# A two-layer gated cross-attention model on one core: heads in pairs, one clip for two heads, float32 weighing in the first layer

## The reference, cut to what matters

```
x = x + tanh(g_xattn[0]) * L0_xattn(layernorm(x), ctx)     # 16 heads of 16
x = x + tanh(g_ffn[0])   * L0_ffn(layernorm(x))            # 8 experts, 3 rotations expm(gens), gate
x = x + tanh(g_xattn[1]) * L1_xattn(layernorm(x), ctx)     # 16 heads of 64
x = x + tanh(g_ffn[1])   * L1_ffn(layernorm(x))            # shared expert + 8 experts

L0_xattn: q, k, v = x@Wq+bq, c@Wk+bk, c@Wv+bv;  attn = softmax(clip(q@k.T/4, -10000, 10000))
          out = (attn @ v) @ Wo + bo
L1_xattn: q, k, v with low-rank additions, from context rows 0..370;  out = softmax(q@k.T/8) @ v
          out += softmax(q@ki.T/8) @ vi    # rows 371..374 with weights Wk_ipa, Wv_ipa
          out = out @ Wo + bo + low-rank part
```

## Time and profile before

| | |
|---|---|
| median of 3 runs (range) | 1279.41 us (1277.0 to 1284.21) |
| profiled execution: span from first to last instruction | 1277.4 us |
| PE (TensorE) busy, matmul | 1066.5 us, 83% |
| PEld (weight loads) busy | 746.0 us, 58% |
| DVE (VectorE) busy | 948.8 us, 74% |
| ACT (ScalarE) busy | 567.6 us, 44% |
| POOL (GpSimd) busy | 268.6 us, 21% |

### The profile page before, as it was taken

The page is one execution under the profiler, slowest core; times in us unless marked ns, Lnnn a source line. Parts: engine busy times, 40 slices in busy tenths (PEclk is TensorE's granted clock), DMA queues, the critical chain, the costliest instruction groups (busy, mean ns, idle before and its releaser), DMA issues.

```text
span 1277.4 us, 23029 instructions
## 1 busy us (share of the span) xinstructions
PE 1066.5 (83%) x7860; PEld 746.0 (58%) x7860; DVE 948.8 (74%) x2024; ACT 567.6 (44%) x1276; POOL 268.6 (21%) x303
## 2 busy tenths in 40 slices
PE   0688888882979999854688988998897699999997
PEld 0577777771634555643367877777776455455553
DVE  5588888897398888697567777777776667776775
ACT  3366666672433343441455556555555233222220
POOL 1422222202245563001000000000000013433331
PEclk9899999995699999896799999999998699999999
DMA  5000000001112122320000000000000231112100
GB/s 190 1 2 2 1 0 0 0 1 66 64 48 84 58 96 67 110 71 28 6 1 2 2 2 1 1 0 1 1 1 1 100 129 64 64 64 72 70 1 29
DMA packets 9935, 47.82 MB, mean 37 GB/s; under 512 B 1513, under 2 KB 3313, under 8 KB 6930
## 3 DMA queue, kind: packets, MB, share of 16 engines
q1 hardware_dynamic: 9874, 47.03, 10.7%
HBM read 45.92 MB, written 1.11 MB: 37 GB/s over the span
## 4 chain that ended last, share of the span: by engine, by line
PE 33%; DVE 30%; issue 20%; ACT 9%; POOL 5%; DMA 2%; DVEq 1%; ACTq 0%; POOLq 0%
PE pb L1119 8%; PE pb L1134 7%; POOL qz L1227 5%; DVE ST L844 4%; DVE ST L855 3%; DVE nm L850 3%; PE pb L640 2%; PE pb L613 2%; PE pb L597 2%; DVE ST L847 2%; ACT ST L728 2%; PE pb L1424 2%; PE pb L576 1%; ACT V L711 1%; PE pb L570 1%
## 5 line engine op out<-in xcount | busy, mean ns | idle before, releaser
L1119 PE MATMUL pb<-xT,KT 128*128 128x448 f16 x1248 | 244.2, 354 | 2.7 <-DVE qz L1197 2.7
L1227 POOL TENSOR_TENSOR qz<-qz,Z 128x448 f32<-128x448 f32 x128 | 169.1, 1331 | 286.8 <-ACT qz L1166 197.5
L1119 PEld LDWEIGHTS pb<-xT,KT 128*128 128x128 f16 x1248 | 121.6, 98 | 119.6 <-DVE qz L1197 5.8
L613 PE MATMUL pb<-KT,qz 128*112 128x375 f16 (+1 forms) x768 | 171.8, 334 | 3.2 <-POOL qz L921 2.1
L640 PE MATMUL pb<-V,ST 125*112 125x32 f16 (+1 forms) x1536 | 127.0, 214 | 53.2 <-DVE ST L855 52.9
L1134 PE MATMUL pb<-V,KT 128*128 128x448 f16 x816 | 162.6, 357 | 8.9 <-DVE V L1206 8.9
L640 PEld LDWEIGHTS pb<-V,ST 125*112 125x112 f16 x1536 | 109.9, 133 | 71.3 <-DVE ST L855 47.2
L736 ACT ACTIVATE ST<-pb 125x336 f16<-125x336 f32 x256 | 113.6, 444 | 45.1 <-PE pb L623 42.5
L855 DVE SCALAR_TENSOR_TENSOR ST<-pb,ST 125x336 f16<-125x336 f32 x256 | 127.7, 499 | 6.0 <-ACT ST L736 5.4
L1134 PEld LDWEIGHTS pb<-V,KT 128*128 128x128 f16 x816 | 80.3, 99 | 86.3 <-DVE V L1206 10.5
L623 PE MATMUL pb<-identf,ST 112*125 112x112 f32 x768 | 125.8, 273 | 1.6 <-ACT ST L728 1.6
(11 more groups left out here) (196 smaller groups left out, 1594.0 us busy)
## 6 DMA issues: line engine op xcount, KB each, us to landing
ST<-in_moe SPq DMA_DIRECT2D x9, 1536.0 KB, 7.8
ST<-in_moe SPq DMA_DIRECT2D x8, 1024.0 KB, 6.8
Z<-wd_scratch SPq DMA_DIRECT2D x16, 448.0 KB, 4.4
ST<-in_ctxT SPq DMA_DIRECT2D x4, 750.0 KB, 4.9
ST<-in_gens SPq DMA_DIRECT2D x2, 768.0 KB, 4.7
ST<-in_lora SPq DMA_DIRECT2D x2, 624.0 KB, 8.7
ST<-in_w1q SPq DMA_DIRECT2D x1, 1024.0 KB
ST<-in_w1k SPq DMA_DIRECT2D x1, 1024.0 KB
```

Source lines behind the costliest of these rows:

```text
L613: mm = pe.matmul(SB_[st % 2][0:S, 0:L.keys], qz[:, bs % 2, qa, h, :], kT[bs % 2][qb][:, h // L.per_tile, 0:L.keys], start=(n == 0), stop=( ...
L1119: mm = pe.matmul(banks[m % len(banks)][:, 0:HT], MW[:, es % 2, qa, c:c + 128], xT[:, qb, k, half * HT:(half + 1) * HT], start=(i == 0), st ...
L1227: pool.tensor_tensor(tile, tile, wdB[:, es % 2, half * HT:(half + 1) * HT], ALU.mult)\
```

## The change

- Heads go in pairs everywhere: both score banks belong to one pair (`SP2`), both transpose banks likewise (`TP2`). TensorE's order in a step is turn of pair p-1, units, weigh of pair p-2, units, scores of pair p+1.
- Layer 1's scores use 64 rows of the array: the two heads of a pair have different halves of the rows, and their matmuls alternate.
- Layer 0: the second clip takes both heads in one instruction; the transposed weights stay float32, written by one ScalarE instruction for both heads, and `lo` is gone there. V is float32 in `V0`, with a 17th column of ones for each head, so that the weighing itself gives the sums; the exponential has no sum. `weigh` is three float32 matmuls of 17 columns for a head, and `normalise` a reciprocal and a multiplication from PSUM. V's units are cut by VectorE alone.
- Layer 1: one maximum, one `hi` and one `lo` for both heads; `normalise` adds the halves in one reduction, and GpSimd divides (`divide`). The factor 16 (`OS`) moves to the `t` unit.
- `at` and `out_at` have new places, SBUF places shift.

```diff
-NORM_LAG = (3, 3)
+NORM_LAG = 2
@@ Layer
-            at = {0: 0, 1: 3, 2: 5, 3: 7, 4: 9, 5: 11}
-            out_at = {0: 5, 1: 8}
+            at = {0: 1, 1: 3, 2: 5, 3: 7, 4: 9, 5: 11}
+            out_at = {0: 5, 1: 13}
...
+            at = dict(enumerate((1, 1, 2, 3, 3, 4, 5, 6, 7, 7, 8, 12, 13, 13, 14, 15, 15)))
+            out_at = {0: 5, 1: 9, 2: 11}
+        order = [0, 4, 1, 5, 2, 6, 3, 7]
+        self.order = list(range(H)) if index else order + [8 + h for h in order]
+        self.pairs = [self.order[2 * p:2 * p + 2] for p in range(NP)]
@@ scores
-                if st >= 2:
-                    pe.wait_ge(s["mx_done0"] if l == 0 else s["exp_done1"], i - 1)
+                if st >= 1:
+                    pe.wait_ge(s["mx_done0"] if l == 0 else s["exp_done1"], 2 * i)
                 for n, (qa, qb) in enumerate(PARTS):
-                    mm = pe.matmul(SB_[st % 2][0:S, 0:L.keys], qz[:, bs % 2, qa, h, :],
-                                   kT[bs % 2][qb][:, h // L.per_tile, 0:L.keys], start=(n == 0), stop=(n == 2))
+                    for j, h in enumerate(L.pairs[p]):
+                        if l == 0:
+                            t, r = h // 8, slice(0, 128)
+                            q = qz[:, bs % 2, qa, h, :]
+                        else:
+                            t, r = h // 2, slice(64 * (h % 2), 64 * (h % 2) + 64)
+                            q = qz[r, bs % 2, qa, h, :]
+                        mm = pe.matmul(SB_[j][0:S, 0:L.keys], q, kT[bs % 2][qb][r, t, 0:L.keys],
+                                       start=(n == 0), stop=(n == 2))
@@ turn
+                if st >= 1:
+                    pe.wait_ge(s["lo_done1"] if l else s["hi_done0"], i)
@@ weigh, layer 0
+                            mm = pe.matmul(psum_out(L, gs, h), PT0[:, st % 2, j, c * S:(c + 1) * S],
+                                           V0[0:CHUNK, bs % 2, c, h, :], start=(c == 0), stop=(c == NCH - 1))
@@ batch of TensorE
-                for h in range(H):
-                    scores(bv, bs, h)
-                    if bs or h >= 2:
-                        turn(bv * H + h - 2, bs * H + h - 2)
...
+                for p in range(NP):
+                    if bs or p >= 1:
+                        turn(bv * NP + p - 1, bs * NP + p - 1)
...
+                    if p >= 2:
+                        weigh(bv, bs, p - 2)
...
+                    if p < NP - 1:
+                        scores(bv, bs, p + 1)
@@ exps, hi
+                    act.activation(P_[:, st % 2, j, :], src, ACT.Exp, bias=nm[:, c:c + 1], scale=-1.0)\
+                        .then_inc(s["exp_done0"], 1)
...
+                act.activation(PT[:, st % 2, :, 0, :] if l else PT0[:, st % 2, :, :], TP2[0:CHUNK, :, 0:NCH * S], ACT.Copy)\
@@ maxima, lo, normalise
+                    for j in range(2):
+                        dve.tensor_scalar(SC[:, st % 2, j, :], SB_[j][0:S, 0:L.keys], -CLAMP, CLAMP, ALU.max, ALU.min,
+                                          accum_out=nm[:, c + j:c + j + 1]).then_inc(s["mx_done0"], 1)
+                    dve.wait_ge(s["mx_done0"], 2 * i + 2)
+                    dve.tensor_scalar(SC[:, st % 2, :, :], SC[:, st % 2, :, :], CLAMP, None, ALU.min)\
...
+                dve.tensor_reduce(nm[:, c:c + 2], SP2[0:S, :, 0:L.keys], AX.X, ALU.max, negate=True)\
...
+                if l == 0:
+                    return
...
+                    dve.reciprocal(rinv[:, heads], whole[:, :, 16]).then_inc(s["r_done0"], 1)
...
+                dve.tensor_reduce(ob, halves, AX.X, ALU.add).then_inc(s[f"halves{l}"], 1)
@@ GpSimd
+                pool.tensor_tensor(ob, ob, bc(rinv[:, heads].unsqueeze(2), [S, L.grouped, L.dim]), ALU.mult)\
+                    .then_inc(s["o_rd1"], 1)
```

## The result

The changed kernel takes 1244.94 us (median of four runs, 1243.78 to 1252.85), the kernel before 1279.09 (1277.0 to 1284.21): the ratio is 0.9746, 95% interval 0.9712 to 0.9781. The forecast was 1227 us, its range 1199 to 1262. The profiled execution has a span of 1242.1 us against 1277.4, 35.3 us less.

What follows compares the result with a forecast made beforehand. The prediction took VectorE to bound the first layer, with TensorE nearly as full, and TensorE the second. From 1277.4 us, -22 and -30 gave 1225 us of span, plus 2.0 the forecast 1227 us; range 1199 to 1262.

Steps and rivals of the forecast that it cites:

- What bounds, and what would: First layer: VectorE sets the pace at 1.27 us a head, TensorE nearly as full; second layer: TensorE itself bounds.
- First layer's batch, 28.3: First layer: a batch falls from 31.0 to 28.3 us, 2.7 less, times 8 = -22 us.
- The weighing: First layer, TensorE: float32 weighing at 0.9 us a pair, from 0.075 us each, the middle of 0.055 and 0.095.
- The 1.3 us added for waits: First layer's batch: 1.3 us for units whose VectorE part stands behind ScalarE's second exponential, and for GpSimd's masks.
- Four passes: First layer's weighing: true float32 as four passes, each at a float16 matmul's cost, 1.3 us a pair; layer gains nothing.
- Second layer's batch, 40.5: Second layer: a batch falls from 44.3 to 40.5 us, 3.8 less, times 8 = -30 us.
- The overlap: Second-layer scores: matmuls of two heads in different row halves run together, 0.48 us a pair in place of 0.96.
- the 0.29 from L600: Second-layer scores: two changes between 128 rows and fewer cost 0.29 us a pair, 0.14 each as read at L600.
- Times 8: Both layers: the gain of one batch multiplied by eight batches, -22 us in the first layer, -30 in the second.
- serial steps: Rival, both layers: one pair in the banks at a time makes each step serial, no change, 1275 us; chance 0.06.
- the first rival: Second layer: the array's halves do not overlap, or the changes cost all; batch stays 44.3, 1257 us; chance 0.17.
- The slower case: Rival, first layer: float32 loads not hidden, 2.3 us a pair, 1309 us; decides from 0.14 us a load; chance 0.08.

Runs made afterwards that it cites:

- experiment 1: Changed kernel with the first layer's float16 weighing in two halves, VectorE's `lo` and ScalarE's accumulator sums back, in pairs: 1262.20 us, ratio 0.9868 to the kernel before.
- experiment 3: Changed kernel with both heads of each second-layer pair in the same half of the rows, so no two halves side by side: 1291.06 us, ratio 1.0069.
- experiment 6: Changed kernel with other slots for the second layer's front units, one unit to a slot from 2 to 14: 1239.05 us, ratio 0.9674.
- experiment 5: Changed kernel with float16 weighing back in the first layer and second-layer scores over all 128 rows; pairs, masks and one clip or maximum stay: 1276.36 us.
- experiment 4: Changed kernel with the first layer's scores also over 64 rows a head, pairs in different halves: 1263.18 us, ratio 0.9858.
- experiment 2: Changed kernel with the second layer's scores over all 128 rows again, still in pairs: 1257.92 us, ratio 0.9820.

## Why the prediction came out as it did

- **What bounds, and what would:** right. VectorE's 1.27 us a head went, and TensorE took over in the first layer; before, TensorE's waits there were for VectorE's `lo`, and with that and the rest of the old weighing back (experiment 1) the batch goes to 30.55 us. That `lo` alone would do it isn't shown.
- **First layer's batch, 28.3:** 28.47, by two errors that cancel. The weighing was mis-sized: 0.9 us a pair forecast, 1.12 measured, 0.093 us a load, which is the price 0.095 that the nearest row (the float32 transpose's load) gave, not the middle that I chose. That is 1.8 us a batch. The 1.3 us added for waits did not come but for 0.3, so the two do not cancel fully: 0.6 us stay that no row here accounts for. The hit is in part luck. From 134 to 276 us, five batches, TensorE waits for ScalarE's exponentials five times, 2.0 us in all, 1.1 of them in the last batch. Scores (1.00 for 0.99), turn (0.64 for 0.66), rounding (0.73 for 0.7) were right; the second clip took 0.55 us or 0.68 under GpSimd's masks.
- **Four passes.** The rule of the Trainium skill ("FP8 and Floating Point Precision", TensorE Precision Notes), priced at float16's 0.055 us, gives an estimate of 1.3 us a pair, as far above the measured 1.12 as my 0.9 is below: a float32 product took 0.187 us, 3.4 times 0.055.
- **Second layer's batch, 40.5:** 40.7. The overlap is real (0.61 us a pair measured, 0.48 + 0.14 forecast), and the two changes of rows cost 0.26 us a pair (experiment 3), near the 0.29 from L600. The Trainium skill's statement that tiles work in parallel ("TensorEngine Tiling", Key Properties), open in the trace before, is borne out by experiment 3: 0.47 us a pair. The maximum took 0.92 for 0.95, GpSimd's division 0.61. TensorE's busy time was 38.45 us for 39.0, and the waits 2.25 us, not 1.5. Of these 1.39 stand at the second unit of a slot, which the change's own new table had put there (experiment 6).
- **Times 8:** this is the step that failed. 2.7 and 3.8 us were multiplied by all eight batches. Six first-layer batches gained 2.5 us each in the mean, the last two together nothing, and the start lost 0.5; in the second layer five gained 3.6, the first 1.05, the last two 1.7, and the start lost 0.2. That makes -14.8 and -20.6 us in place of -22 and -30, hence 1242 in place of 1225 us of span. The last batch, without front units, has another bound: now a pair's loop (3.44 us) in the second layer, and in the first TensorE's own work and a stretch at half clock that costs some 2.2 us. What brings that stretch stays open. Experiment 5 has the longer last batch of the second layer with the pairs alone, so there it comes with them. The second layer's first batch has more waits than the others; why its gain is so small is not shown further.
- **Rivals:** serial steps did not come in ordinary batches, but are what the second layer's last batch shows. Without the overlap of the halves the kernel takes 1291 us (experiment 3), not the 1257 of the first rival, whose sum had no stretches at half clock. The slower case decided from 0.14 us a load on; 0.093 stays clear of it.

## What to carry to other kernels

A gain worked out for the loop's body holds for the body: look up the first and the last pass by themselves, since the work that hides a longer chain is missing in the last. Of a price between two rows take that of the row with the same type and shape, not the middle. When a bound engine is relieved, read the waits of the next one at single instructions: the change's new table of slots, with two units in some, cost 6 us against one unit to a slot, and 15 together with the single maximum.

## What the runs showed of the hardware

- Two float16 matmuls of 64 rows in different halves of the array, with outputs in different banks, start 3 to 4 ns apart; in the same half 156 ns or more apart, as matmuls of 128 rows do. Changing between 128 rows and 64 costs 0.13 us each time (experiment 3), between 128 and one 0.14.
- A float32 weighing of 112 columns of weights and 17 moving ones is two loads and two matmuls for a product, and one such couple issues every 0.093 us.
- The granted clock fell to half in stretches where TensorE was busy (experiment 4, 33.0 us for 27.7 of work) as well as behind a wait of 0.7 us (experiment 2, 43.49 us for 41.8), in some batches and not in others with much the same waits. It moved kernels by as much as their edits did.
- VectorE's SBUF-to-SBUF instructions take longer beside GpSimd's masks: a product of 256 columns, 0.42 us without the masks, took 1.95 us under them (experiment 1), and the changed kernel's clip of 750 columns 0.68 for 0.55, while the rounding remainder from PSUM took 0.85 beside them as elsewhere.
